# An expert layer on one core: the place of a normalization and a transposition in the slab pipeline, and the order of foldings, tables and fills ahead of it

## The chip, the cores and the metric

The kernel runs on 1 core of one Trainium2 chip. The metric is the time of one execution in device microseconds (us). The core has five engines that run their own instruction streams and meet at semaphores: PE (TensorE, the matrix engine), DVE (VectorE), ACT (ScalarE), POOL (GpSimd) and SP (SyncE, which here only issues DMAs).

## The reference

An array `x` of 128 graphs of 128 nodes and 128 features goes through four residual blocks; the last three dots stand for what the change does not touch.

```python
x = x + _L0_gnn_ref(_layernorm(x), adj, ...)      # attention over each graph
x = x + _L0_ffn_ref(_layernorm(x), ...)           # 30 recurrent steps
x = x + _L1_gnn_ref(_layernorm(x), adj, ...)      # graph mixing
x = x + _L1_ffn_ref(_layernorm(x), Wr, br, ln_g, ln_b, W1, b1, W2, b2)
...
# _L1_ffn_ref: 8 experts, 2 of them for each of 128*128 = 16384 tokens
logits = xt @ Wr + br
top_p, top_idx = jax.lax.top_k(softmax(logits), 2)
weights = top_p / top_p.sum(axis=-1, keepdims=True)
xn = (xt - mu) * rsqrt(var + 1e-5)
xe = xn[None] * ln_g[:, None] + ln_b[:, None]
h = gelu(einsum('end,edh->enh', xe, W1) + b1[:, None])     # D = 128, H = 512
y = einsum('enh,ehd->end', h, W2) + b2[:, None]
out = (weights[:, :, None] * y[top_idx]).sum(axis=1)
```

## The kernel before

The 128 graphs are 16 streams of 8 graphs. Everything stays in the on-chip memory until the last block, whose buffers lie over those of the earlier ones.

**The mixing and routing stage** (the loop `for k in range(GNN1_SLOTS)` on each engine, 24 slots) is a software pipeline over the streams, written out in full. In slot k, PE mixes stream k-3, multiplies its rows with the router's weights one slot later (the logits, stream k-4), and counts the tokens of each pair of experts (the ranks, stream k-6, `rank_psum`). DVE routes stream k-5 (`route`, a chain of some 20 small instructions) and finds the place of each token of stream k-7 (`find_slots`, which ends with the cast into `slot` at L813). POOL writes each token's row with its place to the DRAM tensor `sorted_rows`, by 8 indirect DMAs per stream (`scatter`, L538), so that the tokens stand there sorted by the pair of experts that they use.

**The foldings.** `ln_g`, `ln_b`, the mean and `b1` are folded into W1, expert by expert: PE forms the sums for expert e in `psW` (two matmuls, L1206 and L1208), DVE multiplies and adds (L833), which also counts `w1_folded`. Before the change they stand in slots 19 to 22 on PE, two experts a slot, and in slots 20 to 23 on DVE, with two PSUM buffers.

**The tables.** When all slots are done, DVE casts the ends of the pairs' regions to `pad_row` (L845) and computes from them, in some 25 small steps, which pair each slab of 128 sorted rows belongs to. PE turns that (L1214), DVE casts it into `slab_row` and `slab_exp` (L878, L879) and counts `tables_ready`. **The fills**: 29 DMAs write a slab of padding rows behind each pair's region; they read `pad_row`. SP issues 15 and ACT 14 of them (L376), both after `tables_ready`. Then SP waits for all foldings, loads W1 for the first 4 slabs (8 DMAs, L423), waits for the fills and the scatters, and loads the first 7 slabs' rows (L416).

**The expert stage** works on 156 slabs of 128 rows, each with two experts; the queue of each engine is written by hand. The first 12 and last 12 slabs are written out, the 132 between them are a loop on PE, DVE and ACT (12 slabs a turn); POOL's and SP's are written out. For slab n:

- POOL `scale(n)` (L569): one over the deviation of each row, counts `scale_pow`.
- DVE `normalize(n)` (L896): counts `rows_normed`.
- PE `turn(n)` (L1225) transposes, ACT copies back (L1027).
- PE `first_product` (L1235), ACT `gelu` (L1022), PE `second_product` (L1244), each for two experts, counting `y_psum`.
- DVE `finish(n)`: for each of the two experts a register load of the expert's number (`expert_of`, no row of its own in the profile), an addition (L904) and a multiply-add (L909). The second multiply-add counts `y_ready`.
- POOL `store(n)` (L574): an indirect DMA to the output, waits for `y_ready`.

PE's register load for a second product stands between the instruction ahead of it and that product. POOL's queue is: for each n, `scale(n + 4)`, then `store(n)`.

Of the kernel before, what the change touches and what calls it, by code (L numbers as in the profile page):

```python
# [7 lines left out]
I32 = mybir.dt.int32  # L8
U32 = mybir.dt.uint32
F32R = mybir.dt.float32r  # L10
ALU = mybir.AluOpType
# [7 lines left out]
def network(nc, x, adj, W_w, W_b, a_w, a_b, ln_w, ln_b, F_W, F_b, G_w, G_b,  # L19
# [41 lines left out]
    with ExitStack() as ctx:  # L61
# [28 lines left out]
        psW = [psum[:, 2 + j, :] for j in range(2)]  # L90
# [106 lines left out]
        b2_all = over_resid(8, 1).rearrange("p (e d) -> p e d", e=NE)  # L197
        b1_row = over_resid(9, 4).rearrange("p (e h) -> p e h", e=NE)[0:1]
        fold_wide = over_resid(13, 1).rearrange("p (e d) -> p e d", e=NE)
# [80 lines left out]
        pair_tables = sem("pair_tables")  # L280
        centred_logits = sem("centred_logits")
# [69 lines left out]
        GNN1_SLOTS = STREAMS + PLACE_LAG + 1  # L351
# [4 lines left out]
        FOLD_FROM = STREAMS + X3_LAG  # L356
# [13 lines left out]
        def fill(queue, c):  # L370
            if c < PAIRS:
                at = queue.value_load(pad_row[0:1, c:c + 1], min_val=c * REGION, max_val=c * REGION + TOKENS)
                dst = sorted_rows[bass.ds(at, SLAB), :]
            else:
                dst = sorted_rows[PAIRS * REGION:PAIRS * REGION + SLAB, :]
            queue.dma_start(dst, pad[:, :].bitcast(F32)).then_inc(pads_in, 16)  # L376

        @block.sync
        def _(sp):
# [26 lines left out]
            sp.wait_ge(x3_ready, 9)  # L406
            sp.dma_start(b2_all, E_b2.partition_broadcast(P)).then_inc(experts_in[2], 16)
            sp.wait_ge(x3_ready, 13)
            sp.dma_start(b1_row, E_b1.unsqueeze(0)).then_inc(experts_in[3], 16)
# [37 lines left out]
        def _(pool):  # L447
# [82 lines left out]
            for s in range(STREAMS):  # L530
                pool.wait_ge(x2_var_ready, s + 1)
                rsqrt(x_rstd[s % 4][:, :], x_var[s % 4][:, :], x2_pow, s)
                nc.gpsimd.tensor_tensor(values[s], resid[s], wide(x_rstd[s % 4][:, :]), ALU.mult
                                        ).then_inc(x2_scaled, 1)

# [9 lines left out]
            for k in range(STREAMS + SCATTER_LAG):  # L545
                s, m = in_flight(k, 0, SCATTER_LAG)
                if m is not None:
                    pool.wait_ge(x3_pow, m + 1)
                    pool.wait_ge(columns_ready, m + 1)
                    pool.wait_ge(slots_ready, m + 1)  # L550
                    scatter(m, range(TILES // 2))
                if s is not None:
                    c = s % 4
                    if s >= 4:

                        pool.wait_ge(route_step, ROUTE_STEPS * (s - 4) + 1)
                    nc.gpsimd.tensor_copy(state[s][:, :, TOKEN].bitcast(I32), ids[:, s * TILES:(s + 1) * TILES])
# [29 lines left out]
        def _(dve):  # L587
# [226 lines left out]

            dve.wait_ge(pair_tables, 1)
            nc.vector.tensor_copy(pair_end[:, :], region_0[:, :])
            for k in range(GNN1_SLOTS):
# [8 lines left out]
                if k == FOLD_FROM - 1:  # L826
                    dve.wait_ge(x3_ready, 14)
                    nc.vector.tensor_scalar(fold_wide, fold[:, :].unsqueeze(2).to_broadcast([P, NE, D]), 1.0 / D, None,
                                            ALU.mult).then_inc(fold_ready, 1)
                if 0 <= k - FOLD_FROM - 1 < NE // 2:  # L830
                    for e in range(2 * (k - FOLD_FROM - 1), 2 * (k - FOLD_FROM)):
                        dve.wait_ge(fold_psum, e + 1)
                        nc.vector.scalar_tensor_tensor(w1_all[:, e, :], w1_all[:, e, :], params[:, e, 0:1], psW[e % 2],  # L833
                                                       ALU.mult, ALU.add).then_inc(w1_folded, 1)
# [10 lines left out]
            nc.vector.tensor_copy(pad_row[:, :], pair_end[:, :])  # L845
# [29 lines left out]
            last.then_inc(diag_ready, 1)  # L875
            dve.wait_ge(table_psum, 1)
# [4 lines left out]
            last.then_inc(tables_ready, 1)  # L881
            dve.wait_ge(tables_ready, 1)
# [47 lines left out]
        def _(act):  # L930
# [113 lines left out]
        def _(pe):  # L1044
# [91 lines left out]

            for k in range(GNN1_SLOTS):
# [58 lines left out]
                if 0 <= k - FOLD_FROM < NE // 2:  # L1196
                    for e in range(2 * (k - FOLD_FROM), 2 * (k - FOLD_FROM + 1)):
                        if e == 0:
                            pe.wait_ge(fold_ready, 1)
                            pe.wait_ge(experts_in[0], 16)  # L1200
                            pe.wait_ge(experts_in[3], 16)
                        if e < 2:
                            pe.wait_ge(q_copied, STREAMS)
                        else:
                            pe.wait_ge(w1_folded, e - 1)
                        nc.tensor.matmul(psW[e % 2], fold_wide[:, e, :], w1_all[:, e, :], start=True, stop=False,  # L1206
                                         skip_group_check=True)
                        nc.tensor.matmul(psW[e % 2], frac[0:1, :], b1_row[:, e, :], start=False, stop=True,  # L1208
                                         skip_group_check=True).then_inc(fold_psum, 1)
# [5 lines left out]
            last.then_inc(table_psum, 1)  # L1215
            pe.wait_ge(tables_ready, 1)
# [76 lines left out]
```

## Time and profile before

| | |
|---|---|
| median of 3 runs | 2807.94 us (2805.99 to 2810.53) |
| the profiled execution's own time | 2804.9 us |
| its span | 2803.1 us |
| mean granted TensorE clock | 0.97 |
| PE busy | 2489.5 us (89%) |
| DVE busy | 2075.3 us (74%) |
| POOL busy | 2029.8 us (72%) |
| ACT busy | 1809.0 us (65%) |

The span runs from the first to the last instruction of the profiled execution; its own time has 1.8 us around it. Busy shares are averages over stages that are limited by different things: the 30 recurrent steps fill most of the time up to 1660 us, the mixing and routing stage lasts to about 1950 us, and the expert stage starts near 1987 us. PE's clock has two levels, 2.4 GHz (shown as 1.0) and 1.2 GHz (0.5).

### The profile page before, as it was taken

The page shows a single profiled execution, that of the slowest core. Times are in us where ns is not written, and L with a number is a line of the kernel's source. Part 1 is how long each engine was busy: PE and PEld are TensorE (multiplying, and loading weights), DVE is VectorE, ACT ScalarE, POOL GpSimd, SP SyncE. Part 2 cuts the span into 40 slices and gives each one's busy share as a digit, 9 for nine tenths or more (in the row PEclk, how much of TensorE's full clock was granted, in tenths as well). Part 3 has the DMA queues.
Part 4 walks back from the last instruction along what each step waited for, and adds up shares of the span by engine and source line. Part 5 has one row for each costly group of instructions (what it writes and reads, how often), then busy time and mean ns, then how long its engine had stood idle before and what let it go on. Part 6 is the DMA issues. An engine that isn't in the chain of part 4 may idle for free.

```text
span 2803.1 us, 62675 instructions
## 1 busy us (share of the span) xinstructions
PE 2489.5 (89%) x19950; PEld 2340.0 (83%) x19951; DVE 2075.3 (74%) x5754; ACT 1809.0 (65%) x2185; POOL 2029.8 (72%) x1592
## 2 busy tenths in 40 slices
PE   6839999999999999999999999886588888888887
PEld 5839999999999999999999999882577777777777
DVE  6999999999999999999999998674122222222222
ACT  3779999999999999999999973220222222222222
POOL 5779999999999999999999997775232332323323
PEclk9969999999999999999999999995799999999999
DMA  9000000000000000000000000411433333333332
GB/s 267 35 1 1 0 0 0 0 0 0 0 0 0 0 0 0 0 0 0 0 0 0 0 1 32 132 43 49 141 129 125 123 125 125 127 123 126 123 123 76
DMA packets 123642, 141.98 MB, mean 51 GB/s; under 512 B 14951, under 2 KB 76547, under 8 KB 123553
## 3 DMA queue, kind: packets, MB, share of 16 engines
q1 hardware_dynamic: 112450, 122.86, 13.3%
q0 software_dynamic: 9088, 17.14, 1.9%
q10 hardware_dynamic: 2016, 0.95, 0.1%
q8 instruction: 37, 0.61, 0.1%
q14 instruction: 51, 0.42, 0.0%
HBM read 36.35 MB, written 24.58 MB: 22 GB/s over the span
## 4 chain that ended last, share of the span: by engine, by line
DVE 54%; PE 29%; issue 9%; ACT 4%; another core or an unknown queue 2%; SPq 1%; DMA 0%; DVEq 0%; POOL 0%; POOLq 0%; ACTq 0%
DVE pair_stats L639 23%; DVE state L682 17%; PE psum L1244 12%; PE psum L1235 10%; DVE state L661 6%; PE psum L1072 3%; ACT adjT L1022 3%; PE psum L1062 2%; DVE it_vars L643 1%; DVE x_stats L639 1%; DVE resid L709 1%; DVE state L678 1%; DVE resid L669 0%; PE psum L1208 0%
## 5 line engine op out<-in xcount | busy, mean ns | idle before, releaser
L1072 PEld LDWEIGHTS psum<-w_ffn,turned 128*128 128x128 f32 x7680 | 1010.0, 192 | 36.1
L1072 PE MATMUL psum<-w_ffn,turned 128*128 128x128 f32 x7680 | 1013.6, 275 | 0.0
L495 POOL TENSOR_TENSOR it_rstd<-it_vars,minus_half 128x8 f32<-128x8 f32 x480 | 786.3, 1638 | 0.0
L498 POOL TENSOR_TENSOR state<-state,it_rstd 128x768 f32<-128x768 f32 x480 | 708.8, 1477 | 37.7
L639 DVE BATCH_NORM_STATS2 pair_stats<-state 128x6 f32<-128x256 f32 x1920 | 684.9, 417 | 0.0
L1062 PE MATMUL psum<-ident,state 128*128 128x128 f32 x4352 | 596.7, 281 | 72.3 <-DVE state L678 43.0
L574 POOL DMA_INDIRECT out_dram<-resid,adjT x156 | 161.3, 1034 | 554.5 <-DVE resid L909 544.1
L682 DVE SCALAR_TENSOR_TENSOR state<-state,psum 128x1024 f32<-128x1024 f32 x464 | 560.7, 1208 | 1.3 <-ACT state L943 0.7
L1022 ACT ACTIVATE adjT<-psum 128x512 f32<-128x512 f32 x312 | 186.4, 597 | 578.5 <-PE psum L1235 578.4
L1062 PEld LDWEIGHTS psum<-ident,state 128*128 128x128 f32 x4352 | 478.2, 143 | 90.8 <-issue 69.5
L936 ACT COPY turned<-psum 128x1024 f32<-128x1024 f32 x480 | 485.9, 1012 | 78.5 <-PE psum L1062 41.9
L946 ACT ACTIVATE state<-state 128x1024 f32<-128x1024 f32 x480 | 512.7, 1068 | 29.5 <-DVE state L678 9.1
L904 DVE TENSOR_TENSOR resid<-psum,resid 128x128 f32<-128x128 f32 x312 | 91.1, 292 | 543.7 <-PE psum L1244 543.3
L943 ACT ACTIVATE state<-psum 128x1024 f32<-128x1024 f32 x464 | 481.0, 1037 | 0.0
L1244 PE MATMUL psum<-resid,adjT 128*128 x2496 | 352.9, 284 | 109.9 <-ACT adjT L1022 109.9
L1244 PEld LDWEIGHTS psum<-resid,adjT 128*128 128x128 f32 x2496 | 302.1, 191 | 140.2 <-issue 138.3
L1068 PE MATMUL psum<-bias_mv,ones_bf 128*128 128x512 bf16 x992 | 377.8, 381 | 0.2 <-DVE state L757 0.2
L1235 PE MATMUL psum<-resid,adjT 128*128 128x128 f32 x2496 | 332.2, 276 | 0.0
L661 DVE TENSOR_SCALAR state<-state,it_rstd 128x128 f32<-128x128 f32 x960 | 319.7, 373 | 0.0
L1235 PEld LDWEIGHTS psum<-resid,adjT 128*128 128x128 f32 x2496 | 305.4, 193 | 1.2
L538 POOL DMA_INDIRECT sorted_rows<-state,slot x128 | 124.7, 974 | 53.7 <-issue 40.2
L909 DVE SCALAR_TENSOR_TENSOR resid<-resid,adjT 128x128 f32<-128x128 f32 x312 | 109.7, 352 | 23.1 <-DVE resid L904 2.9
(192 smaller groups left out, 1710.0 us busy)
## 6 DMA issues: line engine op xcount, KB each, us to landing
adjT<-resid SPq DMA_DIRECT2D x312, 256.0 KB, 2.3
adjT<-sorted_rows SPq DMA_DIRECT2D x156, 66.5 KB
resid<-in_x_dram SPq DMA_DIRECT2D x16, 512.0 KB, 7.3
state<-in_adj_dram SPq DMA_DIRECT2D x16, 512.0 KB, 7.3
adjT_dram<-adjT SPq DMA_DIRECT2D x7, 512.0 KB, 3.7
adjT<-adjT_dram SPq DMA_DIRECT2D x7, 512.0 KB, 3.5
out_dram<-resid,adjT POOLq DMA_INDIRECT x156, 2.5
sorted_rows<-state,slot POOLq DMA_INDIRECT x128
```

The lines of the kernel that those rows point to most:

```text
L495: nc.gpsimd.tensor_tensor(it_rstd[s % 8][:, :], it_vars[s % 4][:, :], minus_half[:, 0:TILES], ALU.pow).then_inc(it_pow, 1)
L498: nc.gpsimd.tensor_tensor(values[s][:, 0:POOL_TILES, :], values[s][:, 0:POOL_TILES, :], wide(it_rstd[s % 8][:, 0:POOL_TILES]), ALU.mult).t ...
L639: last = nc.vector.bn_stats(dst[:, i, :], src[:, 2 * i:2 * i + 2, :].rearrange("p t d -> p d t"))
L661: last = nc.vector.tensor_scalar(values[r][:, t, :], values[r][:, t, :], it_rstd[r % 8][:, t:t + 1], None, ALU.mult)
L682: nc.vector.scalar_tensor_tensor(values[k], values[k], 0.01, ring[k % 4], ALU.mult, ALU.add).then_inc(state_read, 1)
L936: nc.scalar.copy(turned[s % 4], ring[s % 4]).then_inc(it_turned, 1)
L943: nc.scalar.activation(values[k], ring[k % 4], ACT.Tanh).then_inc(tanh_done, 1)
L946: nc.scalar.activation(values[v], values[v], ACT.Silu).then_inc(silu_done, 1)
L1062: last = nc.tensor.transpose(dst[:, t, :], src[:, t, :], ident[:, :])
L1072: last = nc.tensor.matmul(dst[:, t, :], stationary(t), moving(t), start=bias is None and m == 0, stop=m == len(terms) - 1, skip_group_chec ...
L1235: last = nc.tensor.matmul(psH[o % 4][:, c, :], w1[:, c * P:(c + 1) * P], turned_T[o // 2 % 4], start=True, stop=True)
L1244: last = nc.tensor.matmul(psY[o % 2], hidden[o % 4][:, c, :], w2_all[:, bass.ds(e, 1), c, :].rearrange("p o d -> p (o d)"), start=c == 0, ...
```

## The change

Five things are moved; no arithmetic is added or taken away.

1. **Expert stage, DVE**: `normalize` of slab o+3 stands ahead of `finish` of slab o-1, instead of behind it.
2. **Expert stage, PE**: `turn` stands behind the second product instead of ahead of it.
3. **Foldings**: four PSUM buffers instead of two. PE does experts 0 and 1 in slot 18, 2 and 3 in slot 19, 4 in slot 20, 5 in slot 21, and 6 and 7 behind the tables' matmuls. DVE does 0 to 3 in slots 20 and 21, 4 and 5 behind the tables' steps, 6 and 7 behind `tables_ready`. The loop has 23 slots.
4. **Fills**: start at a new semaphore `ends_ready`, counted by the cast into `pad_row`; SP issues 10 of them ahead of its wait for `tables_ready`, ACT 19. SP loads W1 for two slabs, then rows of three slabs, and the W1 of slabs 2 and 3 between the rows.
5. The token numbers are copied into `state` (POOL, L557 before) when the stream is scaled, 16 copies, instead of between the scatters. `b1_row`, `b2_all` and `fold_wide` change places in memory, and with them the semaphore values at which they are loaded.

```diff
-        psW = [psum[:, 2 + j, :] for j in range(2)]
+        psW = [psum[:, 2 + j, :] for j in range(4)]
...
-        GNN1_SLOTS = STREAMS + PLACE_LAG + 1
+        GNN1_SLOTS = STREAMS + PLACE_LAG
...
-        FOLD_FROM = STREAMS + X3_LAG
+        FOLDS = {18: (0, 1), 19: (2, 3), 20: (4,), 21: (5,)}
+        LATE_FOLDS = (6, 7)
...
             AHEAD = 3
+            sp.wait_ge(ends_ready, 1)
+            for c in range(SP_FILLS):
+                fill(sp, c)
             sp.wait_ge(tables_ready, 1)
-            for c in range(0, PAIRS + 1, 2):
-                fill(sp, c)
             sp.wait_ge(w1_folded, NE)
-            for u in range(8):
+            for u in range(4):
                 load_weights(u)
             sp.wait_ge(pads_in, 16 * (PAIRS + 1))
             sp.wait_ge(scattered, 16 * STREAMS * TILES)
             for n in range(4 + AHEAD):
                 load_rows(n)
+                if n in (2, 3):
+                    load_weights(2 * n)
+                    load_weights(2 * n + 1)
...
+                for e in FOLDS.get(k - 2, ()) if k < GNN1_SLOTS - 1 else ():
+                    fold_weights(e)
...
-            nc.vector.tensor_copy(pad_row[:, :], pair_end[:, :])
+            nc.vector.tensor_copy(pad_row[:, :], pair_end[:, :]).then_inc(ends_ready, 1)
...
             last.then_inc(diag_ready, 1)
+            fold_weights(4)
+            fold_weights(5)
             dve.wait_ge(table_psum, 1)
...
             last.then_inc(tables_ready, 1)
+            for e in LATE_FOLDS:
+                fold_weights(e)
             dve.wait_ge(tables_ready, 1)
...
                 for o in range(EACH):
+                    if not end or o < EACH - 3:
+                        normalize(i, o + 3)
                     if not first or o >= 1:
                         finish(i, o - 1, not first or o >= 5)
-                    if not end or o < EACH - 3:
-                        normalize(i, o + 3)
...
-            act.wait_ge(tables_ready, 1)
-            for c in range(1, PAIRS + 1, 2):
+            act.wait_ge(ends_ready, 1)
+            for c in range(SP_FILLS, PAIRS + 1):
                 fill(act, c)
...
+                elif e >= 4:
+                    pe.wait_ge(w1_folded, e - 3)
...
             last.then_inc(table_psum, 1)
+            for e in LATE_FOLDS:
+                fold_sums(e)
             pe.wait_ge(tables_ready, 1)
...
                     first_product(i, o)
+                    if not first or o >= 2:
+                        second_product(i, o - 2, expert_of(i, o - 2))
                     if o % 2 == 0 and (not end or o < 2 * EACH - 4):
                         turn(i, o // 2 + 2)
-                    if not first or o >= 2:
-                        second_product(i, o - 2, expert_of(i, o - 2))
```

DVE's queue at the start of the expert stage, before: L896 is `normalize` (row_scale0 belongs to slab 4, row_scale1 to slab 5), `ISA` and `TENSOR_LOAD` rows are the register loads, and the pairs of L904 and L909 are the two halves of `finish` of slabs 0 and 1.

```order
L904 TENSOR_TENSOR resid<-psum,resid 128x128
L909 SCALAR_TENSOR_TENSOR resid<-resid,adjT 128x128 [waits y_biased]
L896 TENSOR_SCALAR resid<-adjT,row_scale0 128x128 [waits scale_pow,slab_flip]
L889 TENSOR_LOAD slab_exp
L889 ISA x2
L904 ISA [waits y_psum]
L904 TENSOR_TENSOR resid<-psum,resid 128x128
L909 SCALAR_TENSOR_TENSOR resid<-resid,adjT 128x128 [waits y_biased]
```

The same place with the change (L911 is `normalize`, L919 and L924 are `finish`).

```order
L911 TENSOR_SCALAR resid<-adjT,row_scale0 128x128 [waits scale_pow,slab_flip]
L904 TENSOR_LOAD slab_exp
L904 ISA x2
L919 ISA [waits y_psum]
L919 TENSOR_TENSOR resid<-psum,resid 128x128
L924 SCALAR_TENSOR_TENSOR resid<-resid,adjT 128x128 [waits y_biased]
L904 TENSOR_LOAD slab_exp
L904 ISA x2
L919 ISA [waits y_psum]
L919 TENSOR_TENSOR resid<-psum,resid 128x128
L924 SCALAR_TENSOR_TENSOR resid<-resid,adjT 128x128 [waits y_biased]
L911 TENSOR_SCALAR resid<-adjT,row_scale1 128x128 [waits scale_pow,slab_flip]
```

Before, `finish(0)` is followed by `normalize(4)`; now `normalize(4)` stands ahead of `finish(0)`, and `finish(0)` is followed by `normalize(5)`. POOL's queue, which the change leaves as it is in this stage, has `scale(5)` (row_scale1) behind `store(0)`:

```order
L578 TENSOR_TENSOR row_scale0<-adjT,minus_half 128x1 [waits slab_in4,rows_normed]
L583 DMA out_0_dram<-resid,adjT 16384x128 [waits y_ready]
L578 TENSOR_TENSOR row_scale1<-adjT,minus_half 128x1 [waits slab_in5,rows_normed]
L583 DMA out_0_dram<-resid,adjT 16384x128 [waits y_ready]
L578 TENSOR_TENSOR row_scale2<-adjT,minus_half 128x1 [waits slab_in6,rows_normed]
```

On both lists nothing has moved but what the words above say: DVE's `normalize(n + 5)` now follows `finish(n)`, and POOL's `scale(n + 5)` follows `store(n)` in both kernels.

PE's queue in the same stage, before: behind a first product (L1235) stand the turn (L1225), the register load (L1221) and the second product (L1244).

```order
L1235 MATMUL psum<-resid,adjT 128x128 [waits hidden_ready,slab_turned,w1_in4]
L1235 MATMUL psum<-resid,adjT 128x128 x3
L1225 MATMUL psum<-ident,resid 128x128 [waits rows_normed]
L1221 TENSOR_LOAD slab_exp
L1221 ISA x2
L1244 ISA [waits y_biased,hidden_ready]
L1244 MATMUL psum<-resid,adjT 128x128
```

And with the change (L1255, L1241, L1264, and the turn as L1245, which is the last instruction ahead of the next first product).

```order
L1255 MATMUL psum<-resid,adjT 128x128 [waits hidden_ready,slab_turned,w1_in4]
L1255 MATMUL psum<-resid,adjT 128x128 x3
L1241 TENSOR_LOAD slab_exp
L1241 ISA x2
L1264 ISA [waits y_biased,hidden_ready]
...
L1264 MATMUL psum<-resid,adjT 128x128
L1245 MATMUL psum<-ident,resid 128x128 [waits rows_normed]
L1255 MATMUL psum<-resid,adjT 128x128 [waits hidden_ready,w1_in5]
```

The turn has moved from between two products with a register load behind it to the place behind the second product, with no register load behind it.

DVE's queue at the end of the slots, before: L813 is the last instruction of `find_slots`, L833 a folding, L845 the cast into `pad_row`.

```order
L811 TENSOR_REDUCE rank<-place 128x8 [waits place_step]
L813 CAST slot<-rank 128x8 [waits place_step]
L833 SCALAR_TENSOR_TENSOR resid<-resid,params,psum 128x512 [waits fold_psum] x4
L845 CAST pad_row<-pair_end 128x28
L846 TENSOR_TENSOR pair_steps<-pair_end,region_0 128x28
```

With the change (L822, L856), and further down, where the four foldings (L826) stand now.

```order
L822 CAST slot<-rank 128x8 [waits place_step]
L856 CAST pad_row<-pair_end 128x28
...
L884 TENSOR_TENSOR adjT<-ident,slab_has 128x384
L826 SCALAR_TENSOR_TENSOR resid<-resid,params,psum 128x512 [waits fold_psum] x2
L891 TENSOR_SCALAR slab_row<-psum 128x128 [waits table_psum]
L892 TENSOR_SCALAR slab_exp<-psum 128x2x128
L891 TENSOR_SCALAR slab_row<-psum 128x128
L892 TENSOR_SCALAR slab_exp<-psum 128x2x128
L826 SCALAR_TENSOR_TENSOR resid<-resid,params,psum 128x512 [waits fold_psum] x2
```

Four foldings have moved from ahead of `pad_row` to behind the tables' steps.

## Rows read from the trace of the kernel before

**Rows 1.** Busy time by stretch: PE, PEld, DVE, ACT, POOL (instructions), granted clock, DMA share, GB/s

```profile
1900.00:1950.00 50.00, 38.40 (x83) 13.99 (x83) 22.91 (x93) 1.45 (x3) 33.60 (x35) 0.53 0.14 45
...
2200.00:2300.00 100.00, 81.37 (x631) 73.67 (x632) 29.37 (x95) 27.48 (x57) 31.08 (x40) 1.00 0.36 124
```

**Rows 2.** Timeline, loop of the expert stage: start, duration, engine, line, [idle before <-releaser]

```profile
2302.96 0.35 DVE L909 SCALAR_TENSOR_TENSOR resid<-resid,adjT 128x128 f32<-128x128 f32 x1
...
2303.23 0.34 DVE L896 TENSOR_SCALAR resid<-adjT,row_scale 128x128 f32<-128x128 f32 x1
...
2303.63 0.33 PE L1225 MATMUL psum<-ident,resid 128*128 128x128 f32 x1 [0.26 <-DVE resid L896]
...
2304.14 1.03 POOL L574 DMA_INDIRECT out_dram<-resid,adjT  x1 [3.57 <-DVE resid L909]
...
2304.72 0.97 PEld L1244 LDWEIGHTS psum<-resid,adjT 128*128 128x128 f32 x8 [0.95 <-issue]
...
2305.21 0.58 POOL L569 TENSOR_TENSOR row_scale<-adjT,minus_half 128x1 f32<-128x1 f32 x1
2305.61 0.97 PEld L1235 LDWEIGHTS psum<-resid,adjT 128*128 128x128 f32 x8
...
2306.04 0.29 DVE L904 TENSOR_TENSOR resid<-psum,resid 128x128 f32<-128x128 f32 x1 [2.46 <-PE psum L1244]
2306.43 0.35 DVE L909 SCALAR_TENSOR_TENSOR resid<-resid,adjT 128x128 f32<-128x128 f32 x1
```

**Rows 3.** Timeline, last slabs, written out: DVE alone

```profile
2795.79 0.35 DVE L909 SCALAR_TENSOR_TENSOR resid<-resid,adjT 128x128 f32<-128x128 f32 x1
...
2796.57 0.29 DVE L904 TENSOR_TENSOR resid<-psum,resid 128x128 f32<-128x128 f32 x1 [0.43 <-issue]
2796.89 0.35 DVE L909 SCALAR_TENSOR_TENSOR resid<-resid,adjT 128x128 f32<-128x128 f32 x1
```

**Rows 4.** Timeline, first slabs, written out: a turn and the second product behind it

```profile
2001.91 0.33 PE L1225 MATMUL psum<-ident,resid 128*128 128x128 f32 x1 [0.26 <-DVE resid L896]
...
2002.82 0.97 PEld L1244 LDWEIGHTS psum<-resid,adjT 128*128 128x128 f32 x8 [0.77 <-issue]
```

**Rows 5.** Timeline, loop: the shortest wait of an L904 behind an L909

```profile
2035.69 0.29 DVE L904 TENSOR_TENSOR resid<-psum,resid 128x128 f32<-128x128 f32 x1 [0.68 <-PE psum L1244]
```

**Rows 6.** Timeline, first slabs: a scale and the normalization that waits for it

```profile
1989.26 0.54 POOL L569 TENSOR_TENSOR row_scale<-adjT,minus_half 128x1 f32<-128x1 f32 x1 [0.68 <-DMA adjT<-sorted_rows]
...
1989.91 0.35 DVE L896 TENSOR_SCALAR resid<-adjT,row_scale 128x128 f32<-128x128 f32 x1 [0.88 <-POOL row_scale L569]
```

**Rows 7.** Timeline, end of the slots, foldings and tables

```profile
1927.17 0.39 DVE L808 TENSOR_TENSOR place<-psum,pair_end 128x224 f32<-128x224 f32 x1 [11.41 <-remote]
...
1932.65 0.17 DVE L813 CAST slot<-rank 128x8 int32<-128x8 f32 x1
...
1946.25 0.75 DVE L833 SCALAR_TENSOR_TENSOR resid<-resid,params,psum 128x512 f32<-128x512 f32 x1 [3.26 <-PE psum L1208]
...
1946.92 0.17 DVE L845 CAST pad_row<-pair_end 128x28 int32<-128x28 f32 x1
...
1951.45 0.96 POOL L538 DMA_INDIRECT sorted_rows<-state,slot  x1 [0.31 <-issue]
...
1952.77 2.93 PE L1214 MATMUL psum<-adjT,frac 128*128 128x384 f32 x4 [6.56 <-DVE adjT L873]
...
1956.47 0.41 DVE L879 TENSOR_SCALAR slab_exp<-psum 128x256 int32<-128x256 f32 x1
```

**Rows 8.** Timeline, DMA issues of SP ahead of the expert stage

```profile
1957.89 15.20 SPq L376 DMA_DIRECT2D sorted_rows<-pad  x15
1973.80 9.33 SPq L423 DMA_DIRECT2D adjT<-resid  x8
1983.97 6.98 SPq L416 DMA_DIRECT2D adjT<-sorted_rows  x7
```

**Rows 9.** Timeline, POOL's scatters, 20 in a row: the last of them and its idle time

```profile
1925.18 0.96 POOL L538 DMA_INDIRECT sorted_rows<-state,slot  x1 [0.30 <-issue]
```

More of the change, by code:

```diff
@@ L196, in network @@
         w2_all = over_resid(4, 4).rearrange("p (e c d) -> p e c d", e=NE, c=HC)
-        b2_all = over_resid(8, 1).rearrange("p (e d) -> p e d", e=NE)
-        b1_row = over_resid(9, 4).rearrange("p (e h) -> p e h", e=NE)[0:1]
-        fold_wide = over_resid(13, 1).rearrange("p (e d) -> p e d", e=NE)
+        b2_all = over_resid(13, 1).rearrange("p (e d) -> p e d", e=NE)
+        b1_row = over_resid(8, 4).rearrange("p (e h) -> p e h", e=NE)[0:1]
+        fold_wide = over_resid(12, 1).rearrange("p (e d) -> p e d", e=NE)
         y_out = [over_resid(14, 1)[:, D * q:D * (q + 1)] for q in range(4)]
@@ L280, in network @@
         pair_tables = sem("pair_tables")
+        ends_ready = sem("ends_ready")
         centred_logits = sem("centred_logits")
@@ L376, in fill @@
             queue.dma_start(dst, pad[:, :].bitcast(F32)).then_inc(pads_in, 16)
+        SP_FILLS = 10
         @block.sync
@@ L405, in _ @@
                 sp.dma_start(w2_all[:, e], E_W2[e].rearrange("(c p) d -> p c d", p=P)).then_inc(experts_in[1], 16)
-            sp.wait_ge(x3_ready, 9)
+            sp.wait_ge(x3_ready, 12)
+            sp.dma_start(b1_row, E_b1.unsqueeze(0)).then_inc(experts_in[3], 16)
+            sp.wait_ge(x3_ready, 14)
             sp.dma_start(b2_all, E_b2.partition_broadcast(P)).then_inc(experts_in[2], 16)
-            sp.wait_ge(x3_ready, 13)
-            sp.dma_start(b1_row, E_b1.unsqueeze(0)).then_inc(experts_in[3], 16)
             def load_rows(n):
@@ L534, in _ @@
                                         ).then_inc(x2_scaled, 1)
+                nc.gpsimd.tensor_copy(state[s][:, :, TOKEN].bitcast(I32), ids[:, s * TILES:(s + 1) * TILES])
             def scatter(s, tiles):
@@ L556, in _ @@
                         pool.wait_ge(route_step, ROUTE_STEPS * (s - 4) + 1)
-                    nc.gpsimd.tensor_copy(state[s][:, :, TOKEN].bitcast(I32), ids[:, s * TILES:(s + 1) * TILES])
                     pool.wait_ge(x3_var_ready, s + 1)
@@ L813, in find_slots, with fold_weights @@
                 nc.vector.tensor_copy(slot[:, s, :], rank[:, :]).then_inc(slots_ready, 1)
+            def fold_weights(e):
+                dve.wait_ge(fold_psum, e + 1)
+                nc.vector.scalar_tensor_tensor(w1_all[:, e, :], w1_all[:, e, :], params[:, e, 0:1], psW[e % 4],
+                                               ALU.mult, ALU.add).then_inc(w1_folded, 1)
             dve.wait_ge(pair_tables, 1)
@@ L825, in _ @@
                     route(a)
-                if k == FOLD_FROM - 1:
-                    dve.wait_ge(x3_ready, 14)
+                if k == STREAMS:
                     nc.vector.tensor_scalar(fold_wide, fold[:, :].unsqueeze(2).to_broadcast([P, NE, D]), 1.0 / D, None,
                                             ALU.mult).then_inc(fold_ready, 1)
[L830 to L834, printed above, removed]
+                for e in FOLDS.get(k - 2, ()) if k < GNN1_SLOTS - 1 else ():
+                    fold_weights(e)
             table_at = [0]
@@ L1134, in _, with fold_sums @@
             iteration(STEPS, tail=True)
+            def fold_sums(e):
+                if e == 0:
+                    pe.wait_ge(fold_ready, 1)
+                    pe.wait_ge(experts_in[0], 16)
+                    pe.wait_ge(experts_in[3], 16)
+                    pe.wait_ge(q_copied, STREAMS)
+                elif e == 2:
+                    pe.wait_ge(x3_ready, STREAMS)
+                elif e >= 4:
+                    pe.wait_ge(w1_folded, e - 3)
+                nc.tensor.matmul(psW[e % 4], fold_wide[:, e, :], w1_all[:, e, :], start=True, stop=False,
+                                 skip_group_check=True)
+                nc.tensor.matmul(psW[e % 4], frac[0:1, :], b1_row[:, e, :], start=False, stop=True,
+                                 skip_group_check=True).then_inc(fold_psum, 1)
             for k in range(GNN1_SLOTS):
@@ L1195, in _ @@
                     last.then_inc(logit_psum, 1)
[L1196 to L1209, printed above, removed]
+                for e in FOLDS.get(k, ()):
+                    fold_sums(e)
             pe.wait_ge(diag_ready, 1)
@@ L1215, in _ @@
             last.then_inc(table_psum, 1)
+            for e in LATE_FOLDS:
+                fold_sums(e)
             pe.wait_ge(tables_ready, 1)
```

## The prediction

> **What bounds the kernel now.** I read the busy time by stretch, then the timeline at four places. In the expert stage (150 of its 156 slabs pass one like another) PE is busy 81 of 100 us at the full clock, every other engine a third of the time [rows 1]. DVE's 95 instructions in 100 us, at 5 a slab, are 19 slabs: 5.25 us a slab. The timeline says what a slab of PE is made of [rows 2]: a product takes 0.89 us (from 2304.72 to 2305.61), four of them 3.57; the turn takes some 0.2. The rest is one hole: the turn starts at 2303.63, where it waited for DVE's normalization, and the second product at 2304.72, 1.09 later, with nothing to wait for ("issue"): that is PE's register load, which could not start until the turn had gone. Together with the wait ahead of the turn this is what the change takes away.
>
> Ahead of the stage, DVE ends the last slot at 1932.82, waits for PE's foldings until 1947.00 (4.0 us each: 0.75 of work behind 3.26 of waiting, at half PE's clock), has the tables at 1956.88, and SP issues 15 fills, 8 loads and the first rows at 1983.97, one thing behind another [rows 7, 8].
>
> **The turn and the normalization.** With the turn behind the second product, the register load lies under the first product's 0.89 us. If nothing else bound, a slab would take 3.57 + 0.2 = 3.8 us. But something else does. The order on DVE is now `finish(n)`, `normalize(n+5)`, `finish(n+1)`, and `normalize(n+5)` waits for `scale(n+5)`, which stands on POOL behind `store(n)`, which waits for `finish(n)`. So there is a ring with no slack in it:
>
> - last multiply-add of `finish(n)` to the store's start: 2302.96 to 2304.14, **1.18** [rows 2]
> - store's start to the scale's: 2304.14 to 2305.21, **1.07** [rows 2]
> - scale's start to a normalization that waits for it: 1989.26 to 1989.91, 0.65 [rows 6]; I take **0.62**, since this one has a second semaphore to wait for
> - normalization to the first addition of `finish(n+1)`, with a register load between. The trace has no such pair that doesn't wait for PE. Bounds: 0.78 where the code is written out (2795.79 to 2796.57) [rows 3], and 0.35 + 0.68 = 1.03 for the shortest in the loop, which waited for PE [rows 5]. On PE the same load costs 1.09 in the loop and 0.91 written out [rows 2, 4], so the loop adds 0.18: **0.95**
> - addition to multiply-add: 2306.04 to 2306.43, **0.39** [rows 2]
> - multiply-add to the second addition, the same load again: **0.95**
> - second addition to the last multiply-add: 2796.57 to 2796.89, **0.32** [rows 3]
>
> The sum is 5.48 us a slab, against 5.25: +0.23. PE isn't in this ring: it needs 3.8 of 5.48 us, and a second product may start once the addition two products back is done, at least 3 us ahead of DVE's want of it. Bounds for the ring: with 0.78 for both loads 5.14 (-0.11 a slab), with 1.03 for both 5.64 (+0.39). Over 150 slabs: **+35 us**, between -17 and +59. Where the code is written out both the ring and what it replaces are shorter by a like amount, so I don't part them. What waits behind `normalize` on DVE: both additions, and so PE's second products two further on; ACT, SP and the loads wait for those and have time over.
>
> The Trainium skill gives a register load (`tensor_load`) a floor of about 600 ns (DMA: Bandwidth & Descriptors, "Latency and other measured facts"). The trace shows 0.43 us of idle DVE for load, checks and wait together [rows 3], so by the row it is less here. If that idle time were 0.60, an estimate by that page, the two loads would make the ring 0.34 longer and the change dearer by some 50 us. I go by the row.
>
> **Ahead of the stage.** Four foldings between the last slot and `pad_row` are gone: 1946.92 - 1932.82 = **-14.1 us** [rows 7]. Then, counted from `pad_row`: 5.85 to PE's table matmuls, 2.93 for them [rows 7], two foldings at 4.0 on PE, 0.8 on DVE, 1.0 to SP's first issue (1956.88 to 1957.89), and four loads instead of eight, (1983.97 - 1973.80)/8 = 1.27 each [rows 8]: 23.7 us until the first rows are loaded, instead of 37.05: **-13.4**. The fills are hidden: 19 on ACT at 1.01 us (SP's rate [rows 8]) end at 20, and land before 23. Without that cover each fill more costs 1 us. DVE's foldings 4 and 5 (1.5 us) lie under PE's table matmuls. In the rows that follow, two issue pairs of W1 stand ahead of slab 4's rows: 4 x 1.27 = 5.1 us later, of which PE's and DVE's start-up (the first normalization to the first `finish`, some 8 us) hides about 3.3: **+1.8**. Sum: **-25.7**.
>
> Two folding pairs now stand in slots 18 and 19, ahead of the last ranks and logits. That costs nothing if DVE is as late as now: before `find_slots(14)` it stands idle for 11.41 us, for which the trace names no engine [rows 7]; the semaphore that it awaits is the ranks'. What is late next if that wait goes: POOL, whose scatters (1.27 each [rows 9]) would run on from 1926.14 with 16 more, to 1946.4 instead of 1952.41 [rows 7]. So that wait can give at most 6 to 9 us more, or cost 4 if PE's foldings push the last logits back. I take **-1.5** on the whole. The token copies (16 x 0.2) move on POOL from one full stretch to another: 0, at most 3 either way.
>
> **The sum**, against the profiled execution's own time: 2804.9 + 35 - 25.7 - 1.5 = 2812.7. The median of the runs is 3.0 above that execution (2807.94), so 2815.7; since the ring's unknown is wider upward than down, I say **2817**.
>
> **Rivals.**
> 1. *The ring doesn't bind.* If a scale were done before DVE wants it, PE would set 3.8 us a slab: (3.8 - 5.25) x 150 = -218, with -27: near 2563. For it speaks only the hole on PE. Against it the queue orders: no instruction can pass another on POOL. Chance 0.06.
> 2. *The ring binds, but the gain ahead outweighs it.* The ring at 5.36 (both loads at 0.89) costs 16, and the ranks' wait gives 9 more: 2807.9 + 16 - 34.7 = 2789; with those 9 it decides below a ring of 5.44, without them below 5.39. For it: the two loads are read off by bounds, and one wait has no name. Chance 0.18 for faster by over 0.2%.
> 3. *They cancel*: within 0.2% of before (about what a measurement of this kernel can tell), 2802 to 2813.5: a ring of 5.39 to 5.47. Chance 0.26.
> 4. *PE's clock falls.* It is at 1.0 through the stage with PE busy 81%, and at 0.53 where PE was busy 38 of 50 us with the foldings [rows 1]. With 3.8 of 5.48 us it is busy 69%. At half the clock a slab is 7.6 us of PE: +2.1 a slab for as long as it lasts, +300 in all at the worst; but a slow PE is a busy one. The Trainium skill says that activity is what releases the clock (TensorE: Matmul & The Clock Gate, Part 1); by that rule too a fall should not last. Chance 0.05, at about 2860.
>
> My forecast (ring near 5.48, slower by 0.2 to 1.2%) has 0.45.
>
> **The numbers.** Slower is the forecast and rival 4: 0.50. Same 0.26, faster 0.18 + 0.06 = 0.24. The likeliest case alone spans 2813 to 2842. The range of 8 in 10 takes in rivals 2 and 3 down to 2793 and goes up to 2842.
>
> **What would show it.** In the profile after: POOL's scale directly ahead of each normalization, and the normalization's idle time released by POOL; DVE's first addition of a slab released by nothing ("issue") and no more by PE; the turn without a wait, the "issue" time at the second product gone, PE's wait now for DVE's additions; some 18.2 slabs in 100 us. Ahead of it, `pad_row` directly behind the last slot's cast, SP's first load of rows some 27 us earlier. The prediction is wrong if the normalization doesn't wait for POOL, or if DVE's register load behind a waiting instruction is not the price that I took from its neighbours.

## The result, and the profile after

The changed kernel takes **2865.88 us** (median of 4 runs, 2861.38 to 2868.59) against 2806.97 of the kernel before, measured beside it (2800.12 to 2810.53): a ratio of 1.0211, with an interval of 1.0188 to 1.0235. It is 59 us slower. The prediction said 2817 and a range of 2793 to 2842: the direction was right, the size was not, and the time is outside the range.

Busy time by stretch, the two stretches of [rows 1]:

```profile
1900.00:1950.00 50.00, 37.05 (x86) 15.95 (x87) 27.90 (x120) 1.66 (x5) 32.10 (x33) 0.60 0.30 64
2200.00:2300.00 100.00, 73.21 (x586) 69.95 (x586) 28.42 (x87) 25.89 (x53) 28.25 (x35) 0.97 0.32 110
```

DVE's 87 instructions are 17.4 slabs in 100 us, against 19 before and 18.2 predicted. PE is busy 73 us instead of 81, though its own hole is closed: it now has time over. What sets the slab is seen in the chain that ended last, cut to one slab of the loop (start, us, what; DVEq is DVE's sequencer, and DVEq L904 is the register load and the arithmetic behind it; these rows answer to [rows 2]):

```profile
2231.74 0.08 DVE resid L911
...
2231.86 0.33 DVEq L904
...
2232.22 0.19 DVEq L904
...
2232.72 0.30 DVE resid L919
...
2233.11 0.09 DVE resid L924
...
2233.23 0.57 DVEq L904
...
2234.32 0.30 DVE resid L919
2234.64 0.36 DVE resid L924
...
2235.82 1.04 POOL out_dram L583
...
2236.89 0.59 POOL row_scale L578
2237.51 0.08 DVE resid L911
```

The chain runs from normalization (L911) to normalization over two additions (L919), two multiply-adds (L924), the store (L583) and the scale (L578), and never over PE. It is the ring of the prediction. The steps of this slab: 0.98, 0.39, **1.21**, 0.32, 1.18, 1.07, 0.62, together 5.77. Predicted were 0.95, 0.39, **0.95**, 0.32, 1.18, 1.07, 0.62, together 5.48. One step is clearly off, the one that holds the second register load. This slab is a long one: taken from the start times of 120 slabs between 2050 and 2750 us, the steps are on average 1.00, 0.40, **1.15**, 0.33 and, over store and scale to the next normalization, 2.89. From the 11th store to the 141st a slab takes 5.76 us, against 5.24 in the kernel before.

The same slab in the timeline: both additions are released by nothing ("issue"), and PE's second product waits for the addition, not the other way round.

```profile
2231.74 0.34 DVE L911 TENSOR_SCALAR resid<-adjT,row_scale 128x128 f32<-128x128 f32 x1 [2.51 <-POOL row_scale L578]
2232.22 3.86 SPq L428 DMA_DIRECT2D adjT<-resid  x2
2232.72 0.29 DVE L919 TENSOR_TENSOR resid<-psum,resid 128x128 f32<-128x128 f32 x1 [0.62 <-issue]
...
2233.27 1.15 PE L1264 MATMUL psum<-resid,adjT 128*128 x8 [1.73 <-DVE resid L919]
...
2234.32 0.29 DVE L919 TENSOR_TENSOR resid<-psum,resid 128x128 f32<-128x128 f32 x1 [0.85 <-issue]
```

And the DMA engines from 2233 to 2235, in 40 slices of 0.05 us (busy tenths, then GB/s):

```profile
DMA  0000000649969599998964100600000000000000
GB/s 0 0 0 0 0 0 0 246 164 492 451 246 573 205 451 369 369 451 328 451 246 164 41 0 0 164 0 0 0 0 0 0 0 0 0 0 0 0 0 0
```

A transfer of W1 (the first of the two SPq issues at L428, 256 KB) moves its data from 2233.35 to 2234.15. The register load that began at 2233.23, 0.12 ahead of it, was still running when it started and took 0.57; the one at 2231.86 took 0.33. That suggested a cause, which e7 below tests.

Ahead of the expert stage (answers to [rows 7, 8]):

```profile
1937.54 0.17 DVE L822 CAST slot<-rank 128x8 int32<-128x8 f32 x1
1937.62 0.17 DVE L856 CAST pad_row<-pair_end 128x28 int32<-128x28 f32 x1
...
1947.18 0.42 DVE L892 TENSOR_SCALAR slab_exp<-psum 128x256 int32<-128x256 f32 x1
...
1957.18 0.96 POOL L548 DMA_INDIRECT sorted_rows<-state,slot  x1 [0.30 <-issue]
...
1938.80 22.01 SPq L379 DMA_DIRECT2D sorted_rows<-pad  x10
...
1970.64 2.59 SPq L421 DMA_DIRECT2D adjT<-sorted_rows  x3
...
1938.74 29.66 ACTq L379 DMA_DIRECT2D sorted_rows<-pad  x19
```

`pad_row` stands directly behind the last slot, as foreseen. But that slot ends 4.9 us later than before, and ACT's 19 fills take 29.66 us, 1.56 each, where 1.01 was assumed. That is an average over three stretches of unlike pace: the first eight are issued some 1.1 us apart, with scatters beside them, the next come after 3.57, 4.21 and 6.34 us, and from 1960.5 on, some 2 us behind the end of the last scatter, they are about 1.0 apart again. SP's ten show the same: from the seventh on they are 2.9 to 5.0 apart. SP's first load of rows is at 1970.64, 13.3 us earlier than before, not 27.

### The profile page after: what moved, and what is told of

Read it like the earlier page. It is cut to its first block, busy times and chain, and to the rows that moved or that the text cites. A ratio compares the mean times of both kernels' runs of the same rounds, so it can differ in the third digit from the quotient of the medians.

```text
span 2866.6 us, 62688 instructions
## 1 busy us (share of the span) xinstructions
PE 2466.8 (86%) x19950; PEld 2354.7 (82%) x19951; DVE 2089.8 (73%) x5754; ACT 1812.0 (63%) x2185; POOL 2027.4 (71%) x1592
## 4 chain that ended last, share of the span: by engine, by line
DVE 60%; issue 13%; POOL 9%; DVEq 8%; PE 6%; another core or an unknown queue 2%; ACTq 1%; ACT 1%; SPq 1%; POOLq 0%; DMA 0%
DVE pair_stats L648 23%; DVE state L691 17%; DVEq L904 6%; DVE state L670 6%; POOL out_dram L583 5%; DVE resid L919 3%; POOL row_scale L578 3%; DVE resid L924 3%; PE psum L1087 2%; DVE x_stats L648 2%; DVE it_vars L652 1%; PE psum L1077 1%; DVE resid L718 1%; DVEq L919 1%
## 5 line engine op out<-in xcount | busy, mean ns | idle before, releaser
L583 POOL DMA_INDIRECT out_dram<-resid,adjT x156 | 161.1, 1033 | 626.4 <-DVE resid L924 615.1
L1264 PE MATMUL psum<-resid,adjT 128*128 x2496 | 357.6, 288 | 242.8 <-DVE resid L919 241.8
L1264 PEld LDWEIGHTS psum<-resid,adjT 128*128 128x128 f32 x2496 | 315.6, 198 | 271.0 <-issue 270.6
L911 DVE TENSOR_SCALAR resid<-adjT,row_scale 128x128 f32<-128x128 f32 x156 | 54.0, 346 | 413.7 <-POOL row_scale L578 413.7
L1255 PE MATMUL psum<-resid,adjT 128*128 128x128 f32 x2496 | 343.9, 283 | 0.0
L1255 PEld LDWEIGHTS psum<-resid,adjT 128*128 128x128 f32 x2496 | 317.4, 199 | 0.1
L1042 ACT ACTIVATE resid<-psum 128x128 f32<-128x128 f32 x156 | 43.2, 277 | 399.6 <-PE psum L1245 399.6
L919 DVE TENSOR_TENSOR resid<-psum,resid 128x128 f32<-128x128 f32 x312 | 91.1, 292 | 219.4 <-issue 206.4
## 6 DMA issues: line engine op xcount, KB each, us to landing
adjT<-sorted_rows SPq DMA_DIRECT2D x156, 66.5 KB, 1.7
```

Source lines behind the costliest of these rows:

```text
L1255: last = nc.tensor.matmul(psH[o % 4][:, c, :], w1[:, c * P:(c + 1) * P], turned_T[o // 2 % 4], start=True, stop=True)
L1264: last = nc.tensor.matmul(psY[o % 2], hidden[o % 4][:, c, :], w2_all[:, bass.ds(e, 1), c, :].rearrange("p o d -> p (o d)"), start=c == 0, ...
```

## The experiments

The runs came in three batches, each with its own times of the kernel before: 2806.59 us in e1 to e4, 2777.22 (7 runs, 2775.96 to 2779.41) in e5 to e8, and 2806.16 in e9 to e12. Each run is read against the kernel before in its own batch. A difference between chips is the likely reason, but it is not shown: the record gives the chip number 0 for the first batch and 3 for both others.

**The two halves of the change, and the two halves of its stage.**

```diff
 e1, e4: before, with DVE's order of the change
+                    normalize(i, o + 3)
                     finish(i, o - 1, ...)
-                    normalize(i, o + 3)
 e1, e3: before, with PE's order of the change
-                        turn(i, o // 2 + 2)
                         second_product(i, o - 2, expert_of(i, o - 2))
+                        turn(i, o // 2 + 2)
 e2: the change, with both orders put back
```

> The kernel before with the two edits of the expert stage alone. The changed kernel's loop took 5.75 us a slab against 5.25. Theory A (the ring finish, store, scale, normalize, finish carries all of it): +0.5 x 150 = +75 us, near 2882, and the same 5.7 to 5.8 us a slab. Theory B (the edits ahead of the stage also hurt the loop, for example by a later start of the loads): clearly less than +75. The prediction's ring of 5.48 would give +35, 2842.

Measured 2877.08 us (2872.59 to 2882.41; ratio 1.0263, 1.0242 to 1.0283): +70.5, theory A. That is 0.47 us a slab.

> The kernel before with the edits ahead of the expert stage alone (foldings, tables, fills, loads). In the changed kernel's trace the first finished slab came 10.7 us earlier than before. Theory A: -8 to -12 us, near 2797. The prediction's -27 would give 2780. If nothing ahead of the stage counted: 2807.

Measured 2796.57 (ratio 0.9963, 0.9952 to 0.9975): -10.0. The two halves give +60.5 together, the change had +58.9. So they add up within the noise, and both terms of the prediction were too friendly: +35 was +70, -27 was -10.

> The kernel before with the turn behind the second product, and DVE's order left as it was. Theory A (only DVE's new order makes the ring; PE's hole of 1.1 us was the bound before): the scale of a slab stands ahead of the store that it had to follow, no ring, so PE sets 3.8 to 4.2 us a slab: -150 to -215 us, 2590 to 2660. Theory B (some other chain, over DVE's normalization behind a finish and the turn that waits for it, holds the slab at 5 us or more): 2760 to 2830. Theory C (PE, busier, is throttled): between, with a granted clock under 1.0 for long stretches.

Measured **2587.82** (2579.80 to 2589.48; ratio 0.9219, 0.9195 to 0.9242): -218.8 us, theory A. The same stretch by busy time, and a slab of the timeline:

```profile
2200.00:2300.00 100.00, 99.77 (x892) 99.40 (x891) 41.76 (x135) 39.69 (x81) 43.67 (x54) 1.00 0.52 176
```

```profile
2304.58 0.34 DVE L896 TENSOR_SCALAR resid<-adjT,row_scale 128x128 f32<-128x128 f32 x1
...
2305.45 0.27 PE L1225 MATMUL psum<-ident,resid 128*128 128x128 f32 x1
2305.49 1.03 POOL L574 DMA_INDIRECT out_dram<-resid,adjT  x1 [2.04 <-DVE resid L909]
...
2306.56 0.58 POOL L569 TENSOR_TENSOR row_scale<-adjT,minus_half 128x1 f32<-128x1 f32 x1
...
2308.26 0.34 DVE L896 TENSOR_SCALAR resid<-adjT,row_scale 128x128 f32<-128x128 f32 x1
```

PE is busy all the time, at the full clock, and this slab takes 3.68 us (2304.58 to 2308.26; 3.73 on average from the 11th store to the 141st). The scale still stands behind the store, but the normalization that wants it comes 1.70 us after the scale starts instead of 0.62: it finds it done.

> The kernel before with DVE's order of the change alone, the turn ahead of the second product as before. Theory A (the ring is all on DVE and POOL, the turn isn't in it): 5.7 us a slab as in the changed kernel, +60 to +80, 2867 to 2887. Theory B (the second register load of a slab was longer because PE's changed order put it beside something of PE): 5.48 a slab as predicted, near 2842. If PE's turn joins the ring: more than 2890.

Measured 2875.49 (ratio 1.0263, 1.0237 to 1.0290), the same as e1, so PE's order has no part in the loss. DVE's groups between 2100 and 2500 in this run (busy, mean ns, idle before, releaser):

```profile
L904 DVE TENSOR_TENSOR resid<-psum,resid 128x128 f32<-128x128 f32 x140 | 40.9, 292 | 100.6 <-issue 97.9 <-PE psum L1244 2.7
L896 DVE TENSOR_SCALAR resid<-adjT,row_scale 128x128 f32<-128x128 f32 x70 | 24.2, 346 | 175.7 <-POOL row_scale L569 175.7
```

70 slabs in 400 us are 5.71 us each, and the idle time ahead of the additions is 0.72 on average where 0.60 was predicted. Theory B falls: the longer load is there with PE's old order too.

**Two ways out of the ring.**

```diff
 e5: the change, with DVE's order put back (as e3 against before)
 e6: the change, with POOL's scale a slab earlier
-            for n in range(4):
+            for n in range(5):
                 scale(n)
             for n in range(SLABS):
-                if n + 4 < SLABS:
-                    scale(n + 4)
+                if n + 5 < SLABS:
+                    scale(n + 5)
                 store(n)
```

> The changed kernel with DVE's order put back (normalize behind finish); the turn stays behind the second product, all ahead of the stage stays. Theory A (PE alone bounds the stage once the ring is gone): the time of e3_turn_only less the 10 us of e2_ahead_only, 2578, with 3.7 us a slab. Theory B (the earlier start only moves a wait): 2588, as e3_turn_only.

Measured 2539.13, -238.1 against 2777.22 (ratio 0.9143, 0.9128 to 0.9158). The batch's level explains that it is under 2578; as a difference it is 9 us more than e3 and e2 add up to in the first batch (-228.8), so theory A, with the gain ahead kept.

> The changed kernel, both edits of the stage kept, with POOL's scale one slab earlier: scale(n+5) ahead of store(n) in place of scale(n+4). Theory A (what cost the time is the place of the scale behind the store, not DVE's order by itself): the ring is open, PE bounds the stage, 2570 to 2590. Rival (DVE's order by itself costs, since two additions and two register loads stand behind each normalization): still over 2750, or 5 us a slab.

Measured **2533.82** (2533.44 to 2534.36; ratio 0.9122, 0.9107 to 0.9138), the fastest of all, with both edits of the stage in it. Theory A: what cost the time is one place in POOL's queue, not DVE's order. PE's busy time in the known stretch:

```profile
2200.00:2300.00 100.00, 100.00 (x899) 100.00 (x898) 42.46 (x137) 39.92 (x82) 43.56 (x54) 1.00 0.51 177
```

**The long register load.**

```diff
 e7: the change, where from the ninth W1 transfer on one partition is loaded
-                sp.dma_start(w1_in_use[u % 8], w1_all[:, bass.ds(e, 1), :]...)
+                at = slice(0, P) if u < 8 else slice(P - 1, P)
+                sp.dma_start(w1_in_use[u % 8][at], w1_all[at, bass.ds(e, 1), :]...)
```

> The changed kernel, where from the ninth on a transfer of W1 brings one partition (2 KB) in place of 128 (256 KB), so the experts compute with stale W1; the number of transfers, their issues and their waits stay. In the changed kernel the second register load of a slab on DVE took 0.57 us in most slabs and 0.30 in the rest, and in most of the long ones a W1 transfer was running during the load. Theory A (a register load beside a running W1 transfer takes 0.27 longer): all loads 0.30, 5.45 to 5.5 us a slab, 2820 to 2830. Rival (the load meets SP's own register load or issue, which stay): 0.57 as before, 5.75 a slab, 2860 to 2870.

Measured 2805.14, a ratio of 1.0100 (1.0083 to 1.0117), where the change has 1.0211. The changed kernel was not run in this batch, so the two ratios come from different batches, and the loop is the better witness. The stretch of the chain from the first multiply-add to the second addition (L925 and L920 here, the load is DVEq L905):

```profile
2232.13 0.09 DVE resid L925
...
2232.26 0.30 DVEq L905
...
2233.09 0.30 DVE resid L920
```

0.96 in place of 1.21, and the load is 0.30. The groups of DVE between 2100 and 2500:

```profile
L920 DVE TENSOR_TENSOR resid<-psum,resid 128x128 f32<-128x128 f32 x146 | 42.6, 292 | 88.2 <-issue 88.2
```

An idle time of 0.60 an addition, the predicted one, and 73 slabs in 400 us, 5.48 us each; from the 11th store to the 141st it is 5.51, against 5.76 in the changed kernel and 5.48 predicted. Of that quarter of a microsecond the step with the second load gives back 0.21 (1.15 to 0.94 on average) and the one with the first 0.04 (1.00 to 0.96). The time lies outside the expected 2820 to 2830 either way: 2805 is under it because of the batch's level, and the ratio, put on 2806 us, gives 2834. SP's loads and issues were all still there, so the rival falls: what lengthens the register load is the data of W1's transfer.

It isn't every overlap that does it. Sorted by the first packet of the transfer, all 93 loads of the changed kernel between 2050 and 2750 us that began from 0.2 us ahead of it to 0.1 behind it took 0.54 to 0.59. In the kernel before, 87 loads began 0.35 to 0.45 us behind it, and so inside the transfer too: they took 0.30 to 0.36. The start of the transfer costs the time, not its whole length.

**The fills.**

```diff
 e8: e5, fills of SP and ACT held until the scatters have landed
             sp.wait_ge(ends_ready, 1)
+            sp.wait_ge(scattered, 16 * STREAMS * TILES)
 (the same on ACT)
 e12: e2, fills back behind the tables, dealt out in turn
-            sp.wait_ge(ends_ready, 1)
-            for c in range(SP_FILLS):
-                fill(sp, c)
             sp.wait_ge(tables_ready, 1)
+            for c in range(0, PAIRS + 1, 2):
+                fill(sp, c)
```

> e5_after_norm_back with the fills of SP and ACT held until POOL's last scatter has landed. In the changed kernel the fills began 20 us ahead of the end of the scatters, but some 2 us apart, and near 1.1 us apart behind it. Theory A (fills hardly move beside the scatters, so an early start buys a handful of them): +3 to +7 us on e5_after_norm_back. Rival (they do move, and ACT's 19 fills are the bound by their number): 19 x 1.1 + 1.5 behind 1960 in place of 1970 is 1982, +12 us or more.

Measured 2558.14, 19.0 more than e5: the rival. In this batch fills do move beside the scatters. e5's ACT issues, POOL's last scatter and SP's first load of rows:

```profile
1900.91 19.60 ACTq L379 DMA_DIRECT2D sorted_rows<-pad  x19
```

```profile
1938.26 0.96 POOL L548 DMA_INDIRECT sorted_rows<-state,slot  x1 [0.30 <-issue]
```

```profile
1941.36 2.59 SPq L421 DMA_DIRECT2D adjT<-sorted_rows  x3
```

1.03 us a fill, as predicted, all hidden; the rows wait for the scatters.

> The kernel before, unchanged, for a trace from the same chip as the runs beside it. On the chip of the first traces PE and DVE stood for 4 to 11 us at a time in the slots ahead of the expert stage with no releaser named; on the chip of e5 to e8 the last slot ended 38 us earlier, and the kernel before took 2777 us in place of 2807. Theory A (those standstills belong to the chip that a run gets): the ratio to before is 1, the time one of the two levels, and the end of the last slot goes with it, near 1933 at 2807 or near 1900 at 2777. Theory B (the changed foldings caused or removed them): before ends its slots near 1933 whatever its time.

Measured 2805.34 (ratio 0.9992, 0.9978 to 1.0005): unchanged, as it should be. Its last slot ends at 1929.33, with DVE idle for 3.67, 3.92 and 3.46 us for "remote", where the first trace had 11.41 [rows 7] and 1932.65. The pauses move from one execution to the next. Both theories allow this result: only the kernel before at the level of 2777 us would tell them apart, and it has no trace.

> The changed kernel again. The stage costs +70 us as measured by e1; ahead of it the gain depends on what ends last there. Theory A: on a chip without standstills POOL's scatters end last, 1.27 us each, as far as they go on without a pause, and the ratio to before differs from 1.021 by up to 0.003; on one with them it is again 1.021. Theory B (the fills end last by their number on either): 1.021 on both.

Measured 2867.64, a ratio of 1.0212 (1.0195 to 1.0229), the first result again. Its trace has the slow fills too: 22.07 us for SP's 10 and 29.71 for ACT's 19. The changed kernel itself was not run in the batch of e5 to e8, so the part of the expectation about a chip without standstills stays untested.

> The kernel before with the edits ahead of the expert stage alone, again. Theory A: what it brings is set by the last of three: fills, scatters, foldings. With standstills 10 us as before; without, where the scatters end at 1939 and the kernel before had its foldings and then fills behind the slots, 8 to 20 us.

Measured 2794.35 (ratio 0.9956, 0.9940 to 0.9972): -11.8, as e2.

> e11_ahead_again with the fills put back behind the tables and dealt out to SP and ACT in turn, as before; foldings, loads and token copies as in the change. Theory A (POOL's scatters end last, and fills of 1.0 us each lie beside them wherever they start): within 3 us of e11_ahead_again. Rival (the early start of the fills is what brings the gain): 8 us or more slower than e11_ahead_again.

Measured 2801.65 (ratio 0.9981, 0.9971 to 0.9991): -4.5. It is 7.3 slower than e11, short of the rival's 8. With e11's 5 runs alone the noise leaves theory A's 3 possible; with the 10 runs of e2, the same kernel, the difference is 5.6, and theory A falls. So of the gain ahead some 6 us go with the early start and the dealing out of the fills, the rest with the foldings and loads. Its trace shows the slowdown in miniature: SP's 15 fills took 21.89 us here, from 1956.42 on, with scatters until 1963.16 beside the first of them, against 15.20 for 15 with no scatter beside them [rows 8].

## Why the prediction was wrong

Step by step, as it put them:

- **The ring.** Right in mechanism and order: POOL's scale ahead of each normalization, additions released by "issue", PE's hole gone, PE idle for DVE. The slabs in 100 us were 17.4, not 18.2. One mark is there only in part: the weight load of the second product (PEld L1264) still names "issue", 1.91 us at 2233.26, but it starts 0.25 us behind the end of the addition, for which the matmul's own row names DVE. e3, e4 and e6 show the ring from three sides.
- **"Multiply-add to the second addition, the same load again: 0.95."** This is the step that failed. The term was mis-sized: 1.21 in the slab shown, 1.15 on average. The first load mostly stands clear of the start of a transfer of W1 (0.98, against 0.95), the second mostly meets it. "The same load" was taken for the same price in another place of the slab, and the upper bound of 1.03, a row that waited for PE, lay under the truth. The ring was 5.72 on average (70.5 / 150 = 0.47 above 5.25), not 5.48: 35 us of the 49 that were missed. By e7 some four fifths of that are the second load's.
- **The page's 600 ns.** The prediction set it aside for a row. The Trainium skill's floor for a register load (DMA: Bandwidth & Descriptors, "Latency and other measured facts") is not borne out: 0.30 with no transfer beside it. But 0.57 beside one is near it, and the estimate made from the page, 50 us dearer, would have come to some 2867, the measured time. That would have been luck, since it lengthened both loads of a slab by 0.17, and the first stayed short.
- **"19 on ACT at 1.01 us end at 20, and land before 23": the fills are hidden.** This failed in the result: 29.66 us, so the rows came 33.0 us behind `pad_row` (1937.62 to 1970.64) instead of 23.7. The price of 1.01 was read from fills with nothing beside them [rows 8], and moved to a place beside POOL's scatters. In e5 it held there (1.03), so being beside scatters is not enough to explain it. 9.3 us.
- **"-14.1 for four foldings"**: right; `pad_row` is 0.08 behind the last cast.
- **"-1.5 for the ranks' wait."** In the traces of the result it was +4.9. With the foldings moved the last slot ended at 1937.54, 1936.49, 1939.71 and 1937.24 (after, e10, e2, e11) and at 1944.87 in e12, which has them moved too; where they were not, at 1932.65, 1929.33, 1930.38, 1930.82 and 1941.05 (before, e9, e1, e4, e3). The averages are 6 us apart, against -1.5 forecast, but unchanged code scatters by as much, so how much of it is the edit's own stays open.
- **Start-up, +1.8.** The first finished slab came at 1985.97 (end of its last multiply-add) in place of 1996.6, so 13.3 us at the first load became 10.7 there: +2.6.
- **Rival 4, the clock.** It falls a little, to 0.97 for the stretch from 1.00, but costs next to nothing: PE isn't in the ring, and e7 at 0.98 to 1.00 shows the same ring but for the load.
- **Rival 1** gave 3.8 us a slab and -218 if the ring did not bind. It was dismissed for this kernel, rightly. But the same line of it priced the kernel that should have been made: e3 has -218.8. That it fits to a microsecond is partly luck: e3's slabs take 3.73 us, which would give -226 over 150, and its first normalization came 6.1 us later than in the trace of the kernel before.

So 35 us of the miss come from the ring, most of them from the second load, and some 17 from ahead of the stage, 52 together against the 49 that were missed; e1 and e2 measure them apart (+70.5 for +35, -10.0 for -27).

What stays open: why PE and DVE pause for "remote" in the result and in two batches, and end the slots 38 us earlier, without such a pause, in the batch of e5 to e8 (1899.73 in e5, 1937.54 after); and why fills beside scatters stall behind the first few in the former and go on at 1.03 us in the latter. The pauses and the slow fills go together in the traces here; that they have one cause was not tested. What the start of a transfer does to a register load is measured, not why.

## What to carry to other kernels

When a wait is taken from the engine that bounds a loop, and a second edit goes with it, look in every in-order queue for what stands between the producer and the wait: here one scale behind one store turned a gain of 219 us into a loss of 70, and one place earlier in POOL's queue gave all of it back (-243.4 in its batch). Such a ring shows before a run, as a producer that is queued behind an instruction which waits for the consumer's own previous step; a kernel that has it should be tried with each edit alone. And a duration belongs to its place: when a step moves, ask what runs beside it there, above all which DMA, before its old price is carried along.

## What the hardware showed

- A register load from SBUF took 0.30 us on DVE beside no transfer, and 0.54 to 0.59 when a 256 KB transfer from SBUF to SBUF began from 0.2 us behind the load's start to 0.1 us ahead of it. Of the changed kernel's second loads of a slab between 2050 and 2750 us, 90 of 122 took over 0.5 us in the trace's records, of the first loads 8 of 121. In e7, which removed only the data of these transfers, all 275 recorded loads behind 2050 us took 0.30 to 0.32. In the ring that costs 0.25 us a slab. In the kernel before, the loads met the later part of the transfers and stayed short (87 of them 0.30 to 0.36), so that kernel showed no sign of the price.
- 29 fills of 66.5 KB, issued beside indirect scatters, were about 1.2 us apart for the first six on SP and 1.1 for the first eight on ACT, and then 2.9 to 6.3 us apart until the scatters ended (after, with e10 nearly the same); in e5 the same program ahead of the stage had no stall, 1.03 us each on both. The Trainium skill says that DMAs issued from SP, ACT and POOL share the same 16 engines, and that several issuers save only issue time (Trainium Kernel Development and Optimization, "Key Constraints"). The stall would fit such sharing, but no run here shows that it is the cause, and e5 shows that fills and scatters need not disturb each other.
- The kernel before takes 2777 us in one batch of runs and 2807 in the others, 1% apart, and the last slot ends 38 us earlier in the faster one (e5 against after). A difference of 10 us between kernels is only to be read within one batch.
